# A Mamba layer's side work in single steps: tanh for sigmoid, packed norm factors, gates on GpSimd

## The chip, the cores and the metric

One Trainium2 chip, one of its cores. A core has five engines that run side by side, each with an instruction queue of its own that is worked off in order: PE (matmuls), DVE (vector work), ACT (table functions with a scale and a bias), POOL (GpSimd, general elementwise work) and SP (here for DMAs). They meet through semaphores: an instruction waits until a counter has reached a value. PSUM is the memory that PE writes, in eight banks of 128 rows by 512 fp32; SBUF is the working memory. The metric is the device time of one execution of the whole program, in microseconds (us); the median over several runs counts.

## The reference, cut to what matters

The model has five parts in a row over 2048 tokens of width 128: a gated feed-forward part, a Mamba layer, the feed-forward part again, a mixture of experts, attention, and the experts again. Only the Mamba layer is touched:

```python
hs = layernorm(x)                              # first norm, no weights; the residual too
proj = layernorm(hs) * ln_w + ln_b             # second norm
proj = proj @ in_proj_w + in_proj_b
x1, gate = split(proj, [E])                    # E = 256
x1 = silu(causal_conv(x1, conv_w) + conv_b)    # 4 taps
dt_r, B, C = split(x1 @ x_proj_w, [64, 80])    # rank 64, 16 states
dt = softplus(dt_r @ dt_proj_w + dt_proj_b)
h_t = exp(dt_t * A) * h_{t-1} + dt_t * B_t * x1_t      # for each of 16 states
y_t = sum_n h_t[n] * C_t[n] + x1_t * D
out = (sigmoid(gate) * y) @ out_proj_w + out_proj_b + hs
x = x + out
```

## The kernel before

**Layout.** Channels lie on the 128 partitions and time on the free axis. There are 2 batches of 1024 tokens (SEQ), so 2048 columns, cut into NCH = 4 chunks of 512 (COLS, and HALF within a batch). E = 256 is EB = 2 blocks of 128. The stage is `mamba`, which hands each engine its own list: `mamba_pe`, `mamba_act`, `mamba_dve`, `mamba_pool`. Their order is written out by hand; an engine waits for the others by `wait_ge` on the events named at the top of the file.

**Prelude.** PE forms each chunk's mean (with `mean_mat`, a matrix of 1/128) and DVE subtracts it (`m.hs`). ACT squares, PE forms the variance, the same in all 128 rows. Both norms come from that one variance. For each chunk and each norm ACT takes Ln, Exp (scale -0.5) and Square, and DVE runs a correction step: `second_norm` gives `m.xn`, the input of the projection, and `first_norm` adds the normed residual and the output bias into `c.x`. Batch 0 is then brought through projection, convolution (block 0 as four diagonal matmuls on PE, block 1 as multiply-adds on DVE), SiLU, the rank product (dt's rank, B and C), dt, gate, and the softplus of its block 0. MB_PREP lists these 512-wide products, 16 for batch 0. `first_norm` of chunks 2 and 3 runs on DVE after the first scan.

**Loop.** MB_ITEMS = 64 items: 2 batches x 2 blocks x 16 states. For item i:

```python
# PE:   B of the state spread to 128 rows (b_ps), C likewise in two halves (c_ps, one bank)
# DVE:  u_ps = dtx * b_ps                    (mb_input, L878)
# ACT:  d_a = exp(dt * neg_a)                (mb_decay, L696), two items ahead; copies C (L686)
# DVE:  state = scan(d_a, u_ps)              (mb_scan, L894)
# POOL: state = state * C                    (mb_hc, L920)
# PE:   y_ps += identity @ state             (mb_y, L557), two items later
```

b_ps is single, so PE may spread B of item i+1 only when DVE has multiplied item i; c_ps is one bank, so each half of C waits until ACT has copied the half before. Four decays and four states are held. Between these MB_TICKS places batch 1's products, all in bank 3; a convolution's four taps are spread over three items. Side work of ACT: x, conv, rank, dt and gate outputs (`x_out`, `conv_out`, `rank_out`, `z_out`, `gate_out`), SiLU of batch 1 at item 17, softplus at items 1, 25 and 31 (Abs and Exp, then Ln an item later), the sigmoid of a batch's gate at items 8 and 32. Silu and Sigmoid are in other tables than Exp and Ln, so a table load stands before and after them. POOL forms e - ((1 + e) - 1) and adds it to the logarithm; DVE then adds max(z, 0) (L885) and POOL multiplies dt by x (L916). After 16 items y of a block is complete: DVE's `drain` adds x * D into y_ps (L809) and multiplies by the gate (L813), after which PE may start the next y. `project_out` and `add_out` bring batch 0 out at items 35 to 38.

**Tail.** The last drain, two projections with two matmuls each, and two additions.

## Time and profile before

| | |
|---|---|
| median of 3 runs | 2078.65 us (2077.84 to 2080.35) |
| the profiled execution | 2083.6 us, its span 2082.3 us |
| busy in the span | PE 1859.7, DVE 1396.5, ACT 1128.0, POOL 1168.7 us |
| mean granted TensorE clock | 0.96 of full speed |
| Mamba stage | 161.05 to 505.83 us of the span |

The profile is of one execution. Times of its rows are us from the start of the span; a group gives the mean of one instruction in ns. An engine that is 89% busy over the program may still wait in one stage, so the stage is read by itself. Matmul durations are modelled and overlap: the distance of two starts is the better measure. `x2` at a matmul of fp32 is one product in two passes.

### The profile page before, as it was taken

Reading aid. Unit: us, or ns where it says so; the run is one execution under the profiler, and the core shown is the slowest. Engines: PE = TensorE matmul, PEld = TensorE weight load, DVE = VectorE, ACT = ScalarE, POOL = GpSimd, SP = SyncE. Lnnn points to the kernel's source line nnn. Section 1 sums busy time; section 2 is a strip of 40 time slices with the busy share of each in tenths; the row PEclk is TensorE's granted clock in tenths of the full one; section 3 lists DMA queues with packets and bytes.
Section 4 is the critical chain, followed back from the end, with each engine's and each line's share of the span. In section 5 each row is a group of like instructions: output and inputs, shape, how many; then the busy total and the mean of one; then the engine's idle time right before and its main releaser. Section 6 shows DMA issues by size and latency. Waiting matters only on the chain. (4 is left out here: it accounts for less than half of the span.)

```text
span 2082.3 us, 21845 instructions
## 1 busy us (share of the span) xinstructions
PE 1859.7 (89%) x7336; PEld 1308.0 (63%) x7336; DVE 1396.5 (67%) x2215; ACT 1128.0 (54%) x1586; POOL 1168.7 (56%) x645
## 2 busy tenths in 40 slices
PE   6996788776997994899999999999999999998588
PEld 3773343332775663677777777777777777775366
DVE  5426878896535763567777777777777777774376
ACT  4327667653434444565666566666665666653344
POOL 2450647763543553266666666666666666668354
...
GB/s 91 0 1 0 0 0 1 0 1 0 0 1 45 1 23 82 78 38 75 38 75 42 70 47 66 54 59 54 59 70 43 70 43 68 42 11 11 50 6 16
DMA packets 46048, 74.51 MB, mean 36 GB/s; under 512 B 26864, under 2 KB 28528, under 8 KB 45680
## 3 DMA queue, kind: packets, MB, share of 16 engines
...
q0 software_dynamic: 32, 0.00, 0.0%
...
## 5 line engine op out<-in xcount | busy, mean ns | idle before, releaser
L1994 POOL TENSOR_TENSOR at_e_lo<-at_e,at_e_hi 128x1024 fp32r<-128x1024 f32 x256 | 613.6, 2397 | 381.6 <-DVE at_e_hi L1961 378.8
L1819 ACT ACTIVATE at_e<-at_ps 128x1024 f32<-128x1024 f32 x256 | 263.1, 1028 | 284.3 <-PE at_ps L1726 284.3
L1811 ACT ACTIVATE at_ps<-at_ps,at_neg_diag 128x1024 f32<-128x1024 f32 x256 | 278.6, 1088 | 89.4 <-DVE at_neg_diag L1879 89.4
L1886 DVE TENSOR_REDUCE at_row_max<-at_ps 128x1 f32<-128x1024 f32 x256 | 311.2, 1216 | 5.7 <-PE at_ps L1707 5.7
L1961 DVE CAST at_e_hi<-at_e 128x1024 fp32r<-128x1024 f32 x256 | 257.5, 1006 | 36.9 <-ACT at_e L1819 36.7
L1879 DVE CUSTOM_DVE_ANT_0 at_junk_diag<-at_ps,ident 128x128 bf16<-128x128 f32 x256 | 74.1, 290 | 261.5 <-PE at_ps L1680 261.5
L920 POOL TENSOR_TENSOR mb_work<-mb_work,mb_c 128x1024 f32<-128x1024 f32 x64 | 152.0, 2375 | 147.9 <-DVE mb_work L894 147.1
L386 POOL TENSOR_TENSOR ffn_lo<-ffn_hid,ffn_hi 128x512 fp32r<-128x512 f32 x96 | 124.5, 1298 | 181.7 <-DVE ffn_hi L313 181.7
L1678 PE MATMUL at_ps<-at_k,at_q 128*128 128x512 f32 x512 | 162.9, 400 | 18.8 <-DMA at_k<-at_qk_lo 12.9
L1739 PE MATMUL at_pv_ps<-at_e_hi,at_v_hi 128*128 128x512 f32 x512 | 176.1, 425 | 0.3 <-ACT at_pv_sb L1835 0.3
L1707 PE MATMUL at_ps<-at_k,at_q 128*128 128x512 f32 x512 | 163.5, 401 | 11.5 <-DVE at_row_max L1886 8.1
L1745 PE MATMUL at_pv_ps<-at_e_lo,at_v_hi 128*128 128x512 f32 x512 | 161.8, 397 | 10.1 <-POOL at_e_lo L1994 9.9
L1723 PE MATMUL at_ps<-at_q,at_k 128*128 128x512 f32 x512 | 160.2, 394 | 0.0
L1680 PE MATMUL at_ps<-at_k,at_q 128*128 128x512 f32 x512 | 160.2, 394 | 0.0
L1726 PE MATMUL at_ps<-at_q,at_k 128*128 128x512 f32 x512 | 159.7, 393 | 0.0
L1741 PE MATMUL at_pv_ps<-at_e_hi,at_v_lo 128*64 128x512 f32 x512 | 159.5, 392 | 0.0
L557 PE MATMUL mb_y_ps<-mb_work,ident 128*128 128x512 f32 x256 | 137.9, 624 | 14.1 <-DVE mb_dtx L813 10.5
L894 DVE TENSOR_TENSOR_SCAN mb_work<-mb_work,mb_u_ps 128x1024 f32<-128x1024 f32 x64 | 146.3, 2286 | 5.1
L313 DVE CAST ffn_hi<-ffn_hid 128x512 fp32r<-128x512 f32 x96 | 56.5, 590 | 137.4 <-ACT ffn_hid L287 136.0
L1332 POOL TENSOR_TENSOR moe_hid_lo<-moe_prod,moe_hid_hi 128x512 fp32r<-128x512 f32 (+1 forms) x72 | 92.8, 1290 | 96.2 <-ACT moe_hid_hi L1164 96.2
L686 ACT ACTIVATE mb_c<-mb_c_ps 128x512 f32<-128x512 f32 x128 | 76.3, 596 | 94.1 <-PE mb_c_ps L546 93.3
L1745 PEld LDWEIGHTS at_pv_ps<-at_e_lo,at_v_hi 128*128 128x128 f32 x512 | 94.8, 188 | 51.2 <-POOL at_e_lo L1994 18.4
...
## 6 DMA issues: line engine op xcount, KB each, us to landing
...
```

The costliest lines, as they stand in the source:

```text
L1678: pe.eng.matmul(ps[:, HALF[hf]], q[:, CROSS, rows], k[:, CROSS, HALF[hf]], start=True, stop=False)
L1680: mm = pe.eng.matmul(ps[:, HALF[hf]], q[:, MAIN, rows], k[:, MAIN, HALF[hf]], start=False, stop=True)
L1707: mm = pe.eng.matmul(ps[:, HALF[hf]], q[:, MAIN, blk * P:(blk + 1) * P], k[:, MAIN, HALF[hf]], start=True, stop=True)
L1723: pe.eng.matmul(ps[:, HALF[hf]], k[:, CROSS, keys], q[:, CROSS, HALF[hf]], start=True, stop=False)
L1726: mm = pe.eng.matmul(ps[:, HALF[hf]], k[:, MAIN, keys], q[:, MAIN, HALF[hf]], start=False, stop=True)
L1739: pe.eng.matmul(m.pv_ps[:, HALF[hf]], with_ones, m.e_hi[e % 3][:, HALF[hf]], start=(blk == 0), stop=False)
L1745: mm = pe.eng.matmul(m.pv_ps[:, HALF[hf]], with_ones, m.e_lo[e % 3][:, HALF[hf]], start=False, stop=(blk == BLK - 1))
L1811: act.eng.activation(ps[:], ps[:], ACT.Exp, scale=SCALE, bias=m.small["neg_diag"][s][:, blk:blk + 1], accum_out=m.small["sums"][s][:, blk: ...
L1819: act.eng.activation(m.e[e % 2][:], slot("turned_scores", h, blk)[:], ACT.Exp, scale=SCALE).then_inc(sem["at_exp"])
L1886: dve.eng.tensor_reduce(m.small["row_max"][h % SLOTS][:, blk:blk + 1], slot("best", h, blk)[:], AX.X, ALU.max).then_inc(sem["at_best_out"])
L1961: dve.eng.tensor_copy(m.e_hi[e % 3][:], m.e[e % 2][:]).then_inc(sem["at_hi"])
L1994: pool.eng.tensor_tensor(m.e_lo[e % 3][:], m.e[e % 2][:], m.e_hi[e % 3][:].bitcast(F32), ALU.subtract).then_inc(sem["at_lo"])
```

## The change

- **Norms.** The variance matrix becomes two (`m.pack`), each with 1/128 in 32 columns for the first norm's rows and 32 for the second's; a pair of chunks so lands in one bank, 32 rows each for two chunks and two norms, with an epsilon a row (`m.norm_eps`). ACT takes Ln, Exp and Square once a pair, DVE corrects twice a pair, and PE spreads a row of the result to 128 rows with a selection matrix (`m.sel`, `spread_factor`, event mb_factor). POOL sets these matrices. One DVE step a chunk then gives xn, one the normed residual, kept in `m.hs`. ln_w is multiplied into in_w, and ln_b goes through in_w by four one-column matmuls into in_b. All first norms are in the prelude.
- **Residual.** `project_out` adds `m.hs` by an identity matmul, waited for less than the gated product; `add_out` adds the bias.
- **Batch 0.** Half 1 of block 0's convolution moves from PE to DVE, which works in halves; the logs and the softplus are in halves too. Its four gate products move to items 25 to 28 (MB_TICKS entries now carry the batch).
- **SiLU of batch 1.** Each conv output is Identity, Tanh of half, and a scaling by 0.5 plus 0.5, on ACT, and the product on POOL (MB_SILU).
- **Gate.** Tanh (items 41 to 44) and scaling (45 to 48) by block on ACT; POOL multiplies in halves (`gate_block`, MB_GATE). `drain` is one DVE operation, and y waits for it alone (mb_skip).
- **Tables.** The set that holds Exp and Tanh is loaded at items 5 and 40, the one with Exp and Ln at 17.
- **Softplus.** z_out writes |z| and max(z, 0); 1 + e and 1 - (1 + e) are ACT steps in items of their own, the three sums are POOL's.
- **y** is added three items behind the scan instead of two (MB_Y_LAG); the rest of B and C is formed behind the scan.

```diff
+MB_Y_LAG = 3
...
+    0: (1, 0, None), 1: (1, 1, None), 2: (1, 2, None), 3: (1, 3, None),
...
+    17: (1, 8, None), 19: (1, 9, None), 21: (1, 10, None), 22: (1, 11, None),
+    25: (0, 11, None), 26: (0, 12, None), 27: (0, 13, None), 28: (0, 14, None),
+    29: (1, 12, None), 30: (1, 13, None), 31: (1, 14, None), 32: (1, 15, None), 33: (1, 16, None), 34: (1, 17, None),
 }
-MB_SILU_TICK = 17
-MB_SOFTPLUS_TICK = {1: (0, 1), 25: (1, 0), 31: (1, 1)}
-MB_SIGMOID_TICK = {8: 0, 32: 1}
...
+MB_EXP = {3: (0, 1), 23: (1, 0), 36: (1, 1)}
+MB_ONE_PLUS = {5: (0, 1), 24: (1, 0), 37: (1, 1)}
+MB_ROUNDING = {6: (0, 1), 24: (1, 0), 38: (1, 1)}
+MB_LN = {4: (0, 1), 25: (1, 0), 39: (1, 1)}
+MB_SUMS = ({6: (0, 1), 24: (1, 0), 39: (1, 1)}, {8: (0, 1), 26: (1, 0), 41: (1, 1)}, {10: (0, 1), 28: (1, 0), 43: (1, 1)})
+MB_DTX = {13: (0, 1), 29: (1, 0), 45: (1, 1)}
+MB_SILU = {11: (0, 0), 12: (0, 1), 14: (1, 0), 16: (1, 1)}
+MB_TANH_TABLE, MB_LOG_TABLE = (5, 40), (17,)
+MB_TANH = {41: (0, 0), 42: (0, 1), 43: (1, 0), 44: (1, 1)}
+MB_SIGMOID = {45: (0, 0), 46: (0, 1), 47: (1, 0), 48: (1, 1)}
+MB_GATE = {48: (0, 0), 50: (0, 1), 54: (1, 0)}
+MB_PROJECT = {52: 0, 54: 1}
...
+        pe.eng.matmul(m.var_ps[ch // 2], m.pack[:, ch % 2, :], m.squares[ch],
+                      start=(ch % 2 == 0), stop=(ch % 2 == 1)).then_inc(sem["mb_var"])
...
+        pe.eng.matmul(m.factor_ps[n], m.sel[:, 2 * second + ch % 2, :], m.factor[ch // 2],
...
-            pe.wait_ge(sem["mb_gated"], EB * b + eb)
+            pe.wait_ge(sem["mb_skip"], EB * b + eb)
...
-        pe.wait_ge(sem["mb_gated"], EB * (b + 1))
...
+        pe.eng.matmul(ps, c.ident[:], m.hs[:, COLS[2 * b + h]], start=True, stop=False)
+        pe.wait_ge(sem["mb_gated"], 2 * EB * b + 3 + h)
         for eb in range(EB):
...
+            mm = pe.eng.matmul(ps, c.out_w[:, eb, :], m.dtx[b][:, eb, HALF[h]], start=False, stop=(eb == EB - 1))
...
+    for k in range(2 * EB):
+        mm = pe.eng.matmul(m.banks[7][:, k:k + 1], c.in_w[:, k * P:(k + 1) * P], c.ln_b[:, 0:1], start=True, stop=True)
+    mm.then_inc(sem["mb_mean"])
+    for ch in range(3):
...
+    for ch in range(2):
+        variance(ch)
+    pe.eng.matmul(m.banks[3], c.mean_mat[:], c.x[:, COLS[3]], start=True, stop=True).then_inc(sem["mb_mean"])
+    for ch in range(2, NCH):
+        variance(ch)
+    pe.wait_ge(sem["mb_start"], 2)
+    for n in range(2):
+        spread_factor(n)
...
+        act.eng.activation(m.inverse[pair], m.var_ps[pair], ACT.Ln, bias=m.norm_eps[:, 0:1]).then_inc(logs)
...
+        act.eng.activation(m.inverse[pair], m.inverse[pair], ACT.Exp, scale=-0.5).then_inc(logs)
...
+        act.eng.activation(m.factor[pair], m.inverse[pair], ACT.Square).then_inc(logs)
...
+        act.eng.activation(m.xs[1][:, eb, HALF[h]], mb_bank(m, 1, p), ACT.Identity, bias=c.conv_b[:, eb:eb + 1]).then_inc(out)
+        act.eng.activation(sigmoid, mb_bank(m, 1, p), ACT.Tanh, scale=0.5, bias=m.half_conv_b[:, eb:eb + 1]).then_inc(out)
+        act.wait_ge(out, at + 2)
+        act.eng.activation(sigmoid, sigmoid, ACT.Identity, scale=0.5, bias=0.5).then_inc(out)
...
+        act.eng.activation(m.e_of[g][:, HALF[h]], ps, ACT.Abs, bias=c.dt_b[:, eb:eb + 1]).then_inc(sem["mb_abs"])
+        act.eng.activation(m.dt[b][:, eb, HALF[h]], ps, ACT.Relu, bias=c.dt_b[:, eb:eb + 1]).then_inc(sem["mb_z_out"])
...
+        act.eng.activation(m.dtx[b][:, eb, :], m.e_of[g], ACT.Identity, bias=1.0).then_inc(sem["mb_logs"])
...
+        act.eng.activation(m.dtx[b][:, eb, :], m.dtx[b][:, eb, :], ACT.Identity, scale=-1.0, bias=1.0).then_inc(sem["mb_logs"])
...
+        if i in MB_TANH:
...
-            act.eng.activation(m.gate[b][:], m.gate[b][:], ACT.Sigmoid).then_inc(sem["mb_sigmoid"])
-            load_logs(act)
+            act.eng.activation(m.gate[b][eb], m.gate[b][eb], ACT.Tanh, scale=0.5).then_inc(sem["mb_sigmoid"])
...
+            act.eng.activation(m.gate[b][eb], m.gate[b][eb], ACT.Identity, scale=0.5, bias=0.5).then_inc(sem["mb_sigmoid"])
...
+        dve.eng.scalar_tensor_tensor(m.factor[pair], m.var_ps[pair], m.norm_eps[:, 0:1], m.factor[pair],
+                                     ALU.add, ALU.mult).then_inc(done)
...
+        dve.eng.scalar_tensor_tensor(m.factor[pair], m.factor[pair], 3.0, m.inverse[pair],
+                                     ALU.subtract, ALU.mult).then_inc(done)
...
-        dve.eng.scalar_tensor_tensor(m.xn[:, COLS[ch]], m.hs[:, COLS[ch]], -0.5, m.sq2[ch], ALU.mult, ALU.mult).then_inc(done)
...
-        dve.eng.tensor_scalar(m.xn[:, COLS[ch]], m.xn[:, COLS[ch]], c.ln_w[:, 0:1], c.ln_b[:, 0:1],
...
+        dve.eng.scalar_tensor_tensor(m.xn[:, COLS[ch]], m.hs[:, COLS[ch]], -0.5 * (1.0 + EPS) ** -0.5,
+                                     m.factor_ps[ch], ALU.mult, ALU.mult).then_inc(sem["mb_xn"])
...
+        dve.eng.scalar_tensor_tensor(m.hs[:, COLS[ch]], m.hs[:, COLS[ch]], -0.5, m.factor_ps[NCH + ch],
+                                     ALU.mult, ALU.mult).then_inc(sem["mb_first_norm"])
...
-        dve.eng.scalar_tensor_tensor(m.y_ps[:], m.xs[b][:, eb, :], c.d_skip[:, eb:eb + 1], m.y_ps[:],
+        dve.eng.scalar_tensor_tensor(m.dtx[b][:, eb, :], m.xs[b][:, eb, :], c.d_skip[:, eb:eb + 1], m.y_ps[:],
...
-        dve.eng.tensor_tensor(m.dtx[b][:, eb, :], m.y_ps[:], m.gate[b][:, eb, :], ALU.mult).then_inc(sem["mb_gated"])
...
-        dve.eng.tensor_tensor(c.x[:, COLS[ch]], c.x[:, COLS[ch]], m.c_ps if b and h else m.banks[3],
...
+        dve.eng.scalar_tensor_tensor(c.x[:, COLS[ch]], m.c_ps if b and h else m.banks[3], c.out_b[:, 0:1],
+                                     c.x[:, COLS[ch]], ALU.add, ALU.add).then_inc(sem["x_mamba"])
...
+    for n, (eb, h) in enumerate(((1, 0), (1, 1), (0, 1))):
+        convolve(n, eb, h)
...
+        part = HALF[h]
...
+        dve.eng.tensor_scalar(soft[:, part], m.e_neg[:, part], 1.0, -1.0, ALU.add, ALU.add).then_inc(log1p)
...
+        dve.eng.tensor_tensor(soft[:, part], m.e_neg[:, part], soft[:, part], ALU.subtract).then_inc(log1p)
...
+        dve.eng.tensor_tensor(dt[:, part], dt[:, part], soft[:, part], ALU.add).then_inc(log1p)
+        first_norm(2 + h)
...
-            dve.eng.scalar_tensor_tensor(dt, dt, 0.0, m.log1p, ALU.max, ALU.add).then_inc(sem["mb_dt"])
-        if n == 2 and i > STATES:
-            drain(*mb_part(i - 3)[0:2])
...
+        if n == 3 and i > STATES:
+            drain(*mb_part(i - 4)[0:2])
...
-        if i == 0:
-            for ch in range(2, NCH):
-                first_norm(ch)
+        if (at := mb_product_due(i, 1)) and MB_PREP[at[0]][at[1]][0] == "rank":
+            rest_of_bc(*at)
...
+        for h in range(2):
+            pool.eng.tensor_tensor(m.dtx[b][:, eb, HALF[h]], m.dtx[b][:, eb, HALF[h]], m.gate[b][eb][:, HALF[h]],
+                                   ALU.mult).then_inc(sem["mb_gated"])
...
-            pool.eng.tensor_scalar(m.dtx[b][:, eb, :], m.e_neg, 1.0, -1.0, ALU.add, ALU.add).then_inc(soft)
...
+            pool.eng.tensor_tensor(m.dtx[b][:, eb, :], m.e_of[g], m.dtx[b][:, eb, :], ALU.add).then_inc(soft)
...
+            pool.eng.tensor_tensor(m.dt[b][:, eb, :], m.dt[b][:, eb, :], m.dtx[b][:, eb, :], ALU.add).then_inc(soft)
...
-            pool.eng.tensor_tensor(m.log1p, m.log1p, m.dtx[b][:, eb, :], ALU.add).then_inc(soft)
+            pool.eng.tensor_tensor(m.dt[b][:, eb, :], m.dt[b][:, eb, :], m.log_of[g], ALU.add).then_inc(soft)
...
+            pool.eng.tensor_tensor(m.xs[1][:, eb, HALF[h]], m.xs[1][:, eb, HALF[h]], sigmoid,
+                                   ALU.mult).then_inc(sem["mb_silu"])
...
+    gate_block(BATCH - 1, EB - 1)
```

## Rows read from the trace of the kernel before

**Rows 1.** Table of stretches, whole kernel: start:end, length, then each engine's busy time.

```profile
161.05:209.63 48.58, 33.45 (x67) 13.64 (x67) 33.28 (x53) 38.05 (x57) 2.76 (x3) 0.87 0.00 1
209.63:492.60 282.97, 230.93 (x577) 107.09 (x577) 248.60 (x147) 173.30 (x231) 180.88 (x75) 0.92 0.00 0
492.60:505.83 13.23, 8.13 (x14) 2.69 (x12) 3.89 (x4) 0.00 (x0) 2.34 (x1) 0.87 0.00 0
```

**Rows 2.** DVE's timeline, the loop: start, duration, instruction, idle before it and its releaser.

```profile
209.63 1.23 DVE L878 TENSOR_TENSOR mb_u_ps<-mb_dtx,mb_b_ps 128x1024 f32<-128x1024 f32 x1 [4.89 <-PE mb_b_ps L534]
...
219.42 1.22 DVE L878 TENSOR_TENSOR mb_u_ps<-mb_dtx,mb_b_ps 128x1024 f32<-128x1024 f32 x1
...
242.09 1.23 DVE L878 TENSOR_TENSOR mb_u_ps<-mb_dtx,mb_b_ps 128x1024 f32<-128x1024 f32 x1
...
249.47 1.23 DVE L878 TENSOR_TENSOR mb_u_ps<-mb_dtx,mb_b_ps 128x1024 f32<-128x1024 f32 x1
...
267.71 1.23 DVE L878 TENSOR_TENSOR mb_u_ps<-mb_dtx,mb_b_ps 128x1024 f32<-128x1024 f32 x1 [3.51 <-PE mb_b_ps L534]
...
294.21 1.23 DVE L878 TENSOR_TENSOR mb_u_ps<-mb_dtx,mb_b_ps 128x1024 f32<-128x1024 f32 x1
...
303.88 1.23 DVE L878 TENSOR_TENSOR mb_u_ps<-mb_dtx,mb_b_ps 128x1024 f32<-128x1024 f32 x1 [3.80 <-PE mb_b_ps L534]
...
346.94 1.23 DVE L878 TENSOR_TENSOR mb_u_ps<-mb_dtx,mb_b_ps 128x1024 f32<-128x1024 f32 x1
...
356.64 1.23 DVE L878 TENSOR_TENSOR mb_u_ps<-mb_dtx,mb_b_ps 128x1024 f32<-128x1024 f32 x1
...
368.75 1.23 DVE L878 TENSOR_TENSOR mb_u_ps<-mb_dtx,mb_b_ps 128x1024 f32<-128x1024 f32 x1
...
378.16 1.23 DVE L878 TENSOR_TENSOR mb_u_ps<-mb_dtx,mb_b_ps 128x1024 f32<-128x1024 f32 x1 [0.89 <-PE mb_b_ps L534]
...
399.91 1.23 DVE L878 TENSOR_TENSOR mb_u_ps<-mb_dtx,mb_b_ps 128x1024 f32<-128x1024 f32 x1
...
403.62 1.23 DVE L878 TENSOR_TENSOR mb_u_ps<-mb_dtx,mb_b_ps 128x1024 f32<-128x1024 f32 x1
...
437.04 1.23 DVE L878 TENSOR_TENSOR mb_u_ps<-mb_dtx,mb_b_ps 128x1024 f32<-128x1024 f32 x1
...
443.80 1.23 DVE L878 TENSOR_TENSOR mb_u_ps<-mb_dtx,mb_b_ps 128x1024 f32<-128x1024 f32 x1 [0.89 <-PE mb_b_ps L534]
```

**Rows 3.** Waits of DVE in the loop: us in total, times, longest.

```profile
DVE mb_u_ps L878 <- PE mb_b_ps L534: 20.6, 13, 4.9
```

**Rows 4.** PE's timeline, the loop and the tail.

```profile
281.41 1.02 PE L509 MATMUL mb_c_ps<-mb_conv_in,mb_conv_diag 128*128 128x512 f32 x2
...
285.00 1.02 PE L509 MATMUL mb_c_ps<-mb_conv_in,mb_conv_diag 128*128 128x512 f32 x2
...
423.46 0.73 PE L534 MATMUL mb_b_ps<-mb_bc,pick_r 128*128 128x512 f32 x2 [0.71 <-DVE mb_u_ps L878]
...
440.87 2.04 PE L557 MATMUL mb_y_ps<-mb_work,ident 128*128 128x512 f32 x2 [4.10 <-DVE mb_dtx L813]
...
499.69 5.40 PE L573 MATMUL mb_c_ps<-mb_dtx,out_w 128*128 128x512 f32 x8 [2.64 <-DVE mb_dtx L813]
```

**Rows 5.** Groups of instructions in the loop: busy us, mean ns, idle before.

```profile
L920 POOL TENSOR_TENSOR mb_work<-mb_work,mb_c 128x1024 f32<-128x1024 f32 x63 | 149.6, 2375 | 146.6 <-DVE mb_work L894 145.8 <-ACT mb_c L686 0.8
...
L673 ACT ACTIVATE mb_e_neg<-mb_dt 128x1024 f32<-128x1024 f32 x3 | 3.1, 1049 | 0.0
...
L651 ACT ACTIVATE mb_xs<-mb_c_ps,conv_b 128x512 f32<-128x512 f32 x4 | 2.7, 683 | 0.0
```

**Rows 6.** Groups of instructions in the prelude.

```profile
L781 DVE SCALAR_TENSOR_TENSOR mb_xn<-mb_gate,mb_work 128x512 f32<-128x512 f32 x4 | 2.8, 691 | 0.1
```

**Rows 7.** ACT's timeline, the prelude.

```profile
181.28 1.28 ACT L713 ACT_TABLE_LOAD   x1
182.58 0.69 ACT L713 ACTIVATE mb_xs<-mb_y_ps,conv_b 128x512 f32<-128x512 f32 x1
```

More of the change, by code:

```diff
@@ L464, in mb_part, with mb_log_at @@
+MB_GATE = {48: (0, 0), 50: (0, 1), 54: (1, 0)}
+MB_PROJECT = {52: 0, 54: 1}
+def mb_product_due(i, lag=0):
+    b, p, taps = MB_TICKS.get(i - lag, (None, None, ()))
+    return (b, p) if taps is None or TAPS - 1 in taps else None
+def mb_log_at(b, eb, step):
+    order = sorted((i, n) for n, ticks in enumerate((MB_EXP, MB_ONE_PLUS, MB_ROUNDING, MB_LN))
+                   for i, part in ticks.items() if part == (b, eb))
+    return 4 * (b * EB + eb) + 1 + [n for _, n in order].index(step)
 def mb_part(i):
@@ L467, in mb_part, with mb_last_of_bank @@
     return (*divmod(be, EB), n)
+def mb_last_of_bank(bank, p):
+    return max((k for k in range(p) if MB_BANKS0[k] == bank), default=None)
 def mb_emptied(b, p):
@@ L493, in product @@
         ps = mb_bank(m, b, p)
-        before = (b, p - (1 if b else 4))
-        if b and p == 0:
-            before = 0, max(k for k in range(len(MB_PREP[0])) if k % 4 == 3)
-        if before[1] >= 0:
-            event, count = mb_emptied(*before)
-            pe.wait_ge(sem[event], count)
+        if (b, p) in MB_IN_BANK3[1:]:
+            emptied(*MB_IN_BANK3[MB_IN_BANK3.index((b, p)) - 1])
+        elif (before := mb_last_of_bank(MB_BANKS0[p], p)) is not None:
+            emptied(0, before)
         if kind in ("x", "gate"):
@@ new lines, in mamba_act @@
+    for n, (eb, h) in enumerate(((1, 0), (1, 1), (0, 1))):
+        act.wait_ge(sem["mb_conv_dve"], (n + 1) * TAPS)
+        act.eng.activation(xs[:, eb, HALF[h]], xs[:, eb, HALF[h]], ACT.Silu).then_inc(sem["mb_xs"])
+    load_logs(act)
+    for p in range(5, 7):
+        rank_out(0, p)
+    for h in range(2):
+        z_out(0, 7 + h)
+        act.wait_ge(sem["mb_abs"], h + 1)
+        act.eng.activation(m.e_neg[:, HALF[h]], m.e_neg[:, HALF[h]], ACT.Exp, scale=-1.0).then_inc(sem["mb_logs"])
+    for h in range(2):
+        act.wait_ge(sem["mb_logs"], h + 1)
+        act.eng.activation(m.log1p[:, HALF[h]], m.e_neg[:, HALF[h]], ACT.Ln, bias=1.0).then_inc(sem["mb_logs"])
@@ new lines, in convolve @@
+    def convolve(n, eb, h):
+        conv, out = sem["mb_conv_dve"], m.xs[0][:, eb, HALF[h]]
+        dve.wait_ge(sem["mb_x_out"], 2 * h + 2 - eb)
+        dve.wait_ge(sem["mb_pick"], 2)
+        taps = [m.conv_in[:, eb, k + h * CH:k + (h + 1) * CH] for k in range(TAPS)]
+        dve.eng.tensor_scalar(out, taps[0], c.conv_w[:, eb, 0:1], c.conv_b[:, eb:eb + 1], ALU.mult, ALU.add).then_inc(conv)
+        for k in range(1, TAPS):
+            dve.wait_ge(conv, n * TAPS + k)
+            dve.eng.scalar_tensor_tensor(out, taps[k], c.conv_w[:, eb, k:k + 1], out, ALU.mult, ALU.add).then_inc(conv)
@@ L871, in mamba_dve @@
+    for h in range(2):
+        dve.wait_ge(log1p, 3 * h + 3)
+        dve.wait_ge(sem["mb_logs"], 2 + h + 1)
+        dve.eng.tensor_tensor(dt[:, HALF[h]], dt[:, HALF[h]], m.log1p[:, HALF[h]], ALU.add).then_inc(log1p)
+    dve.wait_ge(log1p, 8)
+    dve.eng.tensor_tensor(soft, dt, m.xs[0][:, 0, :], ALU.mult).then_inc(log1p)
+    dve.wait_ge(log1p, 9)
+    dve.wait_ge(sem["mb_norm"], 4)
+    dve.wait_ge(sem["mb_first_norm"], NCH)
+    dve.wait_ge(sem["mb_factor"], 2 * NCH)
     for i in range(MB_ITEMS):
```

455 lines of the change are left out of this document (231 added, 224 removed), and 6 rows, old and new, of the table MB_TICKS.

## Prediction

> **What bounds it now.** First the table of stretches [rows 1]: the Mamba stage is 344.8 us of the 2082.3 (prelude 48.6, loop over 64 items 283.0, tail 13.2); the diff touches nothing else and no DMA. In the loop DVE is busy 248.6, PE 230.9, ACT 173.3, POOL 180.9. Next, DVE's timeline [rows 2]: an undisturbed item starts 3.71 after the one before (399.91 to 403.62), and 64 of them are 237.4. The loop takes 282.97, 45.6 more. Taking 3.71 an item from the differences of those starts shows where: item 0 6.1, items 1 to 5 4.1, item 6 3.7, items 7 to 10 3.4, 11 to 17 0.5, 18 6.0, 19 to 29 2.2, 30 6.0, 31 to 33 1.0, 34 5.7, 35 to 39 3.2, 40 to 49 nothing, 50 3.0, 51 to 63 0.6. Then DVE's waits [rows 3]: 20.6 of it is B's broadcast from PE; most of the rest is DVE's own extra work. Last, PE's timeline [rows 4]: in a plain item PE idles 0.71 before it may overwrite B, and with one extra fp32 matmul its round is 3.59 (281.41 to 285.00). So DVE bounds the loop, PE is second with little room, POOL and ACT matter where they hold one of these up. The prelude is a chain through all four engines.
>
> **The loop, part by part** (excesses from the timeline [rows 2]).
> Removed: (a) item 0's 6.1: two first norms behind the first scan, now in the prelude. (b) At items 6, 30 and 36 DVE adds the softplus parts; with late decays and POOL's dtx behind the second these are 3.7, 7.0 and, of the 3.2 at 35 to 39, 1.5. POOL takes them: -12.2. (c) At item 10 DVE waits 3.51 for B: PE stood behind ACT's copies of C, those behind the sigmoid and its two table loads, 4.5 on ACT. Tanh needs none between decays: -3.4. (d) A drain is two DVE operations of some 1.25, and PE's next y waits for both. The three cost 6.0 (with SiLU's two loads and a rank product), 6.5 (with a late y) and 3.4. DVE keeps one operation, 1.2 over the floor.
> Left of the drains: before the third, PE idled 4.10 and then ran a matmul pair in 2.04, where 285.00 shows 1.02 [rows 4]; B came 0.89 late. The idle becomes 2.9. If the clock holds, a drain costs 1.2, and 2.1 at item 19, where a rank product of two matmuls stands before B; if it drops as now, 1.1 more, and at item 19 another 2.3. I take the drop, the nearest shown case: 4.4, 2.3, 2.3 = 9.0, bounds 4.5 and 9.0.
> Start-up: items 1 to 5 cost 4.1; ACT will again copy x, and exp, ln, 1+e and the tanh load come at items 3 to 5: 3, bounds 1 and 6.
> Convolution: 16 diagonal matmuls of 0.85 in items 4 to 15. PE's round with two is 4.45, with one 3.59, so twelve items need 1.7 more than DVE, which PE's lead takes, as now (0.5 at items 11 to 17). New on ACT: each of the four outputs is three operations of 0.6 to 0.69 where one was 0.68 [rows 5], ahead of a copy of C that PE needs only after the next product and B. Within the 3.
> The rest of B and C (0.72 twice, 2.2 now with its waits) moves behind the scan: 1.4. project_out gets the residual as a third matmul, so PE's rounds 52 and 54 are 2.74 + 2.55 = 5.3; three rounds need 13.3 where DVE gives 11.1: 2.2, DVE's two additions inside, bounds 1.3 and 4.
> Batch 0's four gate products now lie in items 25 to 28, rounds of 3.59 under DVE's 3.71; without that cover 3.4.
> Softplus on ACT: 1+e and its rounding are two more steps of 1.05 [rows 5] a block; tanh and its scaling are four each. ACT's plain item takes 2.3 of 3.71, a copy of C may come some 2 late. Only items 5 and 24 get more than that: 1.0, bounds 0 and 5.
> POOL: sums of 2.36, as before but for one of 3.6; new are four SiLU halves (1.3) and the gates (2.6 a block). It has 3.71 - 2.38 = 1.33 free an item [rows 5]; the worst pile (items 11 to 14) makes it 1.7 late, and with MB_Y_LAG 3 y asks for its product one item later. Nothing.
> Left over the floor: 9.0 + 3 + 1.4 + 2.2 + 1.0 = 16.6 instead of 45.6. **Loop -29.0.**
>
> **The prelude.** Counted from 161.05 with 0.72 a DVE half step [rows 6], 0.66 an ACT half step and 1.28 a table load [rows 7], 0.9 an fp32 matmul. The four bias products are eight weight loads, some 1.6; one-column matmuls are not in the trace, so the bounds are nothing and 3.6 (four full ones). Means and centres then come 0.8 later; the fourth mean stands behind two variances, its centre ends at 168.7, the eight diagonals at 170.6. Ln, Exp, Square of the first pair are done at 169.1, under them. POOL's twelve memsets ahead of the spreading, at 0.92 each (2.76 for three [rows 1]), end by 172.1. Two factor steps end 172.0, spreading 172.95, xn of chunks 0 and 1 173.7 and 174.6, the second factor 176.0, three half convolutions of 2.7 (0.5 and three of 0.73) 184.1. SiLU of the last half 184.8, table 186.1, two rank outputs 188.5, Abs, Relu and Exp of both halves 192.0. DVE has first norms 0 and 1 done at 191.55, behind PE's spreads and dt products. Two halves of softplus with a first norm each, 2.56 a half, end 196.7, two log additions 198.1, dt times x 199.4. B is there by 193.5. PE stands idle several times before that, and after such a stretch a pair takes twice as long [rows 4]: I add 0.9. Item 0 starts at 200.3 against 209.63: **prelude -9.3**, bounds -13 (ACT's and DVE's halves overlap fully) and -4 (half clock in every spread and rank product, bias products at 3.6). What goes is four gate products ahead of B (4.89 of waiting before the first multiply [rows 2]), a convolution on PE, and 24 ACT half steps of the norms, now six.
>
> **The tail.** Drain 1.28, then POOL's first gate half 1.3 instead of DVE's 1.22. The residual matmul of half 0 is hidden by them, that of half 1 is not: +0.9. But the idle before the projections shrinks from 2.64 to 1.9, and their eight passes, 5.40 now [rows 4], are 3.5 at full clock. Bounds -1.0 and +1.9, I take +0.5.
>
> **Table loads against the notes.** A load of 1.28 is followed by its ACTIVATE 1.30 after its own start [rows 7]. The Trainium skill, "ScalarE: Activation LUTs", section "What ACT_TABLE_LOAD costs", adds a drain of 1380 ns to each switch, 2.66 us in all. The trace disagrees: nothing lies between. By the page the loop's loads, six now and three after, would be worth another 4.1 us of ACT.
>
> **Sum.** -29.0 - 9.3 + 0.5 = -37.8. The profiled execution took 2083.6 (span 2082.3) and would take 2045.8. It lies 4.95 above the median of 2078.65, so the median becomes 2040.9, rounded to 2041.
>
> **Rivals.**
> *ACT in part exposed.* The 4.5 block of item 10 was exposed by 3.4, so 1.1 fits unnoticed. The four conv outputs (1.9), items 5 (2.3) and 24 (2.1), and pairs with x, dt or gate outputs (1.6) exceed that. Where PE has no lead each loses up to 1.2, eight of them 10: 2051. For: PE's round of 3.59. Against: items 19 to 29 hold single steps of 1.05 now and are 2.2 over, 2.1 of it the rank items.
> *The prelude does not shorten* by more than 1: it gets three more PE round trips (variance pair, factor, spread). 2049.
> *ACT fully exposed, slower.* Between the copies of C stand 20 wide steps of 1.06 (21.2), the conv outputs (7.4), and x, dt, gate, rank outputs and loads (17.7): 46.3. If each delays C, so B, so DVE by its whole length, less the 4 counted above, it is 2041 + 42 = 2083. It decides when 38 of the 46 are exposed, so only if PE never regains a lead; plain items give 0.71 each.
> *Loads come back.* If each tanh draws its own load and each decay the other, as silu and sigmoid do now, 8 groups x 2 x 1.28 = 20.5 on ACT, some 12 exposed: 2053. Against: Silu's four in a row draw one.
> *Less left over.* The clock holds at the drains and ACT hides: 4.5 + 1 + 1.4 + 1.3 = 8.2 over the floor (loop -37.4), prelude -11, tail +0.5: 2031.
>
> **How the numbers follow.** Forecast 0.70 (its own range 2034 to 2048), ACT in part 0.10, prelude 0.05, loads 0.03, less left over 0.06, ACT fully exposed 0.04, and 0.02 for a sum of these that comes out level. A measurement here tells 0.2%, 4 us, from no change. Faster 0.94, same 0.02, slower 0.04. The range takes in the less-left-over and the partly exposed cases: 2030 to 2054.
>
> **What would show it.** Right: the first multiply some 39 after the stage's start; a loop near 254; plain items at 3.71; no log1p addition on DVE in the loop; lone table loads at items 5, 17 and 40; waits for B below 10. Wrong: DVE waiting for B in most items of 4 to 16 and 23 to 48 with ACT the releaser of C; scans waiting for y (lag 3, four states held); the half clock for longer than now.

## The result, and the profile after

The new kernel takes 2041.18 us, median of 4 runs (2039.14 to 2043.06), the old one 2079.5 beside it: a ratio of 0.9816, 95% interval 0.98 to 0.9831. Forecast were 2041 and 2030 to 2054. The table of stretches of the new kernel (columns as in [rows 1]), prelude, loop and tail:

```profile
159.10:198.46 39.36, 32.44 (x76) 13.82 (x76) 28.26 (x53) 25.50 (x39) 5.38 (x15) 0.94 0.00 1
198.46:452.54 254.08, 225.76 (x587) 105.83 (x588) 230.90 (x135) 182.19 (x251) 188.96 (x85) 0.97 0.00 0
452.54:465.06 12.52, 8.34 (x19) 2.98 (x17) 2.78 (x4) 0.00 (x0) 4.82 (x3) 1.00 0.00 0
```

Against [rows 1] the prelude is 9.2 shorter (forecast 9.3), the loop 28.9 (29.0), the tail 0.7 (0.5 longer). Together the stage is 38.8 shorter in the two profiled executions; the medians lie 38.3 apart. DVE's work in the loop fell by 17.7 and its waits for B from 20.6 [rows 3] to 11.4 ("below 10" was one of the signs named for being right: that one missed); ACT's and POOL's work grew by 9 and 8, and both are still less busy than DVE. DVE's waits in the loop:

```profile
DVE mb_u_ps L980 <- PE mb_b_ps L595: 11.4, 12, 2.3
DVE mb_u_ps L980 <- DVE mb_work L989: 0.9, 2, 0.5
DVE mb_work L989 <- PE mb_y_ps L616: 0.6, 3, 0.3
```

Take 3.71 an item from the differences of the multiplies' starts, as before. The excess is 16.6, as forecast, but otherwise divided:

| items | forecast | measured |
|---|---|---|
| 0 to 17 (start-up, convolution) | 3 | 5.8 |
| 19, 35, 51 (drains) | 9.0 | 2.3 + 1.8 + 1.8 = 5.9 |
| 18, 20 (rest of B and C) | 1.4 | 1.3 |
| 52 to 55 (output) | 2.2 | 2.9 |
| others | 1.0 | 0.7 |

An item is counted from its own multiply to the next one. 2.3 of the first line is one item, 7. DVE's timeline there, then PE's and ACT's of the same time:

```profile
226.09 1.23 DVE L980 TENSOR_TENSOR mb_u_ps<-mb_dtx,mb_b_ps 128x1024 f32<-128x1024 f32 x1
...
232.12 1.23 DVE L980 TENSOR_TENSOR mb_u_ps<-mb_dtx,mb_b_ps 128x1024 f32<-128x1024 f32 x1 [2.33 <-PE mb_b_ps L595]
```

```profile
224.81 1.03 PE L595 MATMUL mb_b_ps<-mb_bc,pick_r 128*128 128x512 f32 x2
226.01 0.50 PE L606 MATMUL mb_c_ps<-mb_bc,pick_r 128*128 128x512 f32 x1 [0.17 <-ACT mb_c L784]
...
227.53 0.50 PE L606 MATMUL mb_c_ps<-mb_bc,pick_r 128*128 128x512 f32 x1 [0.17 <-ACT mb_c L784]
...
229.64 1.98 PE L548 MATMUL mb_c_ps<-mb_conv_in,mb_conv_diag 128*128 128x512 f32 x4 [0.75 <-ACT mb_e_neg L736]
231.06 1.03 PE L595 MATMUL mb_b_ps<-mb_bc,pick_r 128*128 128x512 f32 x2
```

```profile
223.00 1.05 ACT L766 ACTIVATE mb_dtx<-mb_dt 128x1024 f32<-128x1024 f32 x1
224.07 1.28 ACT L112 ACT_TABLE_LOAD   x1
225.36 0.60 ACT L784 ACTIVATE mb_c<-mb_c_ps 128x512 f32<-128x512 f32 x1
...
226.89 0.59 ACT L784 ACTIVATE mb_c<-mb_c_ps 128x512 f32<-128x512 f32 x1
227.37 1.06 ACT L770 ACTIVATE mb_dtx<-mb_dtx 128x1024 f32<-128x1024 f32 x1
228.32 0.69 ACT L735 ACTIVATE mb_xs<-mb_c_ps,conv_b 128x512 f32<-128x512 f32 x1
228.89 0.70 ACT L736 ACTIVATE mb_e_neg<-mb_c_ps,mb_half_conv_b 128x512 f32<-128x512 f32 x1
```

Read backwards: the multiply waits for B (L595); B stands on PE behind the second convolution's first matmuls (L548); these wait for bank 3, which ACT empties with the second step of the first output (L736); and that step comes late behind the rounding (L770). Before that, PE had stood twice in front of a half of C (L606), because ACT copies the half before (L784) late behind 1+e (L766) and the table load.

How much is whose follows from the distance of two B's. At item 10, where PE waits for nobody, it is 4.53 with a product of two matmuls:

```profile
238.26 1.03 PE L595 MATMUL mb_b_ps<-mb_bc,pick_r 128*128 128x512 f32 x2
...
241.41 1.95 PE L548 MATMUL mb_c_ps<-mb_conv_in,mb_conv_diag 128*128 128x512 f32 x4
242.79 1.02 PE L595 MATMUL mb_b_ps<-mb_bc,pick_r 128*128 128x512 f32 x2
```

At item 7 it is 6.25, so 1.7 more: by the starts between, some 0.8 at the two halves of C and 0.9 at the bank. The other 0.6 of item 7, and the 0.6 of items 10 and 13, are PE's own round of 4.53 against DVE's 3.71; rounds with one matmul, 3.60, give PE only 0.1 of lead each. Item 4's 0.6 is such a round with a wait of 0.17 for ACT; item 17's comes with the rank product's two matmuls, PE waiting 0.5 and 0.2 for copies of C before them; item 1's 0.9 falls where PE, after an idle of 4.1, runs at a granted clock of 0.50 (199.0 to 206.5).

The drains: PE's timeline at items 19 and 35, the y pair behind the drain, what stands between, and B.

```profile
278.13 1.10 PE L616 MATMUL mb_y_ps<-mb_work,ident 128*128 128x512 f32 x2 [1.14 <-DVE mb_dtx L913]
279.06 1.88 PE L558 MATMUL mb_c_ps<-mb_xs,x_w 128*128 128x512 f32 x4
280.38 1.03 PE L595 MATMUL mb_b_ps<-mb_bc,pick_r 128*128 128x512 f32 x2
...
340.68 2.05 PE L616 MATMUL mb_y_ps<-mb_work,ident 128*128 128x512 f32 x2 [2.84 <-DVE mb_dtx L913]
341.74 1.84 PE L595 MATMUL mb_b_ps<-mb_bc,pick_r 128*128 128x512 f32 x2
```

At 35 (and 51) the idle is the 2.9 forecast and the pair takes 2.05: the granted clock from 340.5 to 343.5 is 0.50, the lower level, 1.2 GHz. At 19 PE came late itself, idled only 1.14, and the clock held: 1.00, 2.4 GHz, from 277.9 to 281.4. The four other profiles with 1.14 to 1.18 of idle before such a y (softplus earlier, PE kept busy, lag 2, gates ahead of B) had the pair at full speed too.

### The profile page after: what moved, and what is told of

It reads as the page before. It is cut to its first block and busy times, and to the rows that moved or that the text cites. A ratio compares the mean times of both kernels' runs of the same rounds, so it can differ in the third digit from the quotient of the medians.

```text
span 2037.7 us, 21921 instructions
## 1 busy us (share of the span) xinstructions
PE 1844.3 (91%) x7360; PEld 1301.5 (64%) x7360; DVE 1374.8 (67%) x2202; ACT 1124.5 (55%) x1587; POOL 1183.9 (58%) x669
## 3 DMA queue, kind: packets, MB, share of 16 engines
HBM read 20.93 MB, written 1.18 MB: 11 GB/s over the span
## 5 line engine op out<-in xcount | busy, mean ns | idle before, releaser
L1944 ACT ACTIVATE at_e<-at_ps 128x1024 f32<-128x1024 f32 x256 | 263.0, 1028 | 281.4 <-PE at_ps L1851 281.4
L390 POOL TENSOR_TENSOR ffn_lo<-ffn_hid,ffn_hi 128x512 fp32r<-128x512 f32 x96 | 124.6, 1300 | 173.0 <-DVE ffn_hi L317 173.0
L616 PE MATMUL mb_y_ps<-mb_work,ident 128*128 128x512 f32 x256 | 131.9, 602 | 8.3 <-DVE mb_dtx L913 6.8
L1803 PEld LDWEIGHTS at_ps<-at_k,at_q 128*128 128x128 f32 x512 | 95.2, 189 | 47.2 <-DMA at_k<-at_qk_lo 14.9
```

Source lines behind the costliest of these rows:

```text
L1803: pe.eng.matmul(ps[:, HALF[hf]], q[:, CROSS, rows], k[:, CROSS, HALF[hf]], start=True, stop=False)
L1944: act.eng.activation(m.e[e % 2][:], slot("turned_scores", h, blk)[:], ACT.Exp, scale=SCALE).then_inc(sem["at_exp"])
```

## The experiments

Each changes the new kernel only as its diff says. The loop's length, from each trace, is the finest measure, but not a perfect one. Of items that no edit reaches most repeat within 0.1 from kernel to kernel; items 1 to 4 together (1.5 in the new kernel, 1.2 in most, 0.05 in "drain twice") and items 35, 36, 51 and 52 (by up to 0.9 each) move with PE's clock (last section). The new kernel's loop is 254.1, and that of "PE kept busy", whose edit does not reach the loop, 253.6: a difference of 0.5 says nothing.

**Loads back** (the rival "Loads come back").

```diff
+        load_tanh(act)
         act.eng.activation(sigmoid, mb_bank(m, 1, p), ACT.Tanh, ...)
+        load_logs(act)
...
```

The same stands around the gates' tanh; the loads at items 5, 17 and 40 are gone.

> The new kernel, with each of the eight tanh steps (four in the convolution's outputs, four on the gates) preceded by a load of tanh's table set and followed by a load of the decays' set: 16 loads of 1.28 us and none of the three at items 5, 17, 40, so 13 more, 16.6 us of ScalarE. Theory A (ScalarE's long work in the batch-1 convolution is exposed, as item 7's 2.33 us of waiting for B shows; from item 41 on ScalarE has 1.4 us free in each item and a gate tanh alone takes 1.05): the four convolution groups become 1.9 + 2.56 = 4.5 us long, and each costs about 2 more, the gates' groups 3.6 us long in consecutive items and some 4 in all: the loop 254.1 becomes 266, the run about 2053, as the rival in the prediction has it. Theory B (PE's lead hides it, only blocks above 4.5 us show): the loop grows by under 4, the run is 2041 to 2045.

Measured: 2058.38 us, ratio 0.9897 (0.9881 to 0.9914), loop 272.8: 18.7 longer, more than the 16.6 of ACT added. Items 7, 10, 13, 17 cost 4.5, 2.1, 2.1, 4.7, item 19 4.0, items 43 to 46 7.4. ACT's time is exposed almost one for one wherever its item is full. Item 17 adds to it: PE waits 3.18 there for a copy of C behind the last conv output, and its matmuls behind that idle, and again behind the one of 2.43 at item 19, run partly at the lower clock (granted 0.59 and 0.66). PE never waits for POOL in this loop. The rival's price, 12, was too low.

**Softplus earlier**, to thin out the pile before item 7.

```diff
-MB_EXP = {3: (0, 1), ...};  MB_ONE_PLUS = {5: (0, 1), ...}
+MB_EXP = {2: (0, 1), ...};  MB_ONE_PLUS = {3: (0, 1), ...}
```

> The new kernel with ScalarE's softplus exp of the first block at item 2 instead of 3 and its 1+e at item 3 instead of 5; the tanh table load stays at item 5. Theory A (item 7's excess of 2.32 us is ScalarE's pile of 1.05 + 1.28 + 1.06 + 1.9 us in items 5 to 7, which holds up the copies of C, so B): item 7's excess falls to 1.0 or less, items 1 to 4 may gain up to 0.6, items 0 to 17 together cost 4.3 over the floor instead of 5.84, the run is 1.5 us shorter. Theory B (it is PE's own work in items 4 to 7, convolution matmuls ahead of B, or the four convolution operations): item 7 stays at 2.2 or more and the run at 2041.

Measured: 2039.8, ratio 0.9809 (0.9792 to 0.9825), loop 253.5, which is no shorter than with no edit in it (253.6). Item 7 fell from 2.3 to 1.5, item 4 rose by 0.4. Between the two: at item 7 PE no longer waits for a copy of C, but still 0.74 for the bank, because the rounding still stands before the output. So 1+e had cost 0.8 by way of C; the rest is the bank and PE's own round.

**B before y** at the drains.

```diff
+        late = i >= STATES and n == 3
-        if i >= MB_Y_LAG:
+        if i >= MB_Y_LAG and not late:
             add_to_y(i - MB_Y_LAG, 0)
...
             spread_b(i + 1)
             spread_c(i + 1, 1)
+        if late:
+            add_to_y(i - MB_Y_LAG, 0)
```

> The new kernel with PE's order changed at items 19, 35 and 51 alone: the next item's B and C go ahead of the first half of y, which has to wait for DVE's drain there. Theory A (DVE waits 1.26, 0.89 and 0.89 us for B behind y at the three drains, and PE's half clock matters only for what DVE waits for): these waits go, each drain costs 1.2 to 1.3 (its own DVE operation and start), the loop is 2.5 to 3.0 shorter, 251.3. Theory B (PE's two halves of y then collide with the next round and the wait moves to the next item's B or to the scan's wait for y): the three drains together stay at 5 or more of 6.0 and the run at 2041.

Measured: 2036.2, ratio 0.9792 (0.9776 to 0.9808), loop 249.3, 4.8 shorter. Items 19, 35, 51 cost 1.1, 1.0, 1.0, so 2.7 less, as Theory A says, and item 52 fell from 1.8 to 0.3, which it had not seen. That is 4.3 for the edit; the other 0.5 lies in items 1 and 4, which it doesn't reach. PE's timeline at item 35 of this kernel:

```profile
337.62 0.73 PE L595 MATMUL mb_b_ps<-mb_bc,pick_r 128*128 128x512 f32 x2 [1.56 <-DVE mb_u_ps L983]
...
338.89 3.17 PE L616 MATMUL mb_y_ps<-mb_work,ident 128*128 128x512 f32 x4 [0.31 <-DVE mb_dtx L916]
```

The y's at 35 still run slow (3.17 for four records, 1.88 at item 19), but the B that DVE needs next is no longer behind them.

**PE kept busy** in the prelude.

```diff
     for ch in range(2, NCH):
         variance(ch)
+        pe.wait_ge(sem["mb_centred"], 2)
+        pe.eng.matmul(m.banks[1], c.mean_mat[:], c.x[:, COLS[1]], start=True, stop=True)
```

> The new kernel with two extra matmuls in the prelude, one behind each of the last two variances, into a bank that nobody needs then: they fill PE's idle stretches of 0.90 and 0.99 us ahead of the first spreading matmuls, which in the new kernel took 3.44 us for a pair and at other places 1.88. Theory A (the pair is slow because the clock had fallen to its lower level after PE's idle stretches, which the extra work prevents): the pair takes about 1.9, the first normed chunk is ready 0.6 to 0.9 earlier and the loop's first multiply comes about 1 us earlier. Theory B (the clock is low there whatever PE does, or something else holds it): the pair stays at 3.4, the extra work adds up to 0.4, the first multiply is at the same place or later.

Measured: 2041.08, ratio 0.9813 (0.9797 to 0.983); first multiply 37.88 after the stage's start, 39.36 in the new kernel. But two of the three kernels above, which don't have the edit, showed 37.9 too, and the median is that of the new kernel, so this run alone decides nothing (last section).

**Product behind B**, and then **outputs behind C** on top of it.

```diff
-        if i in MB_TICKS:
-            product(*MB_TICKS[i])
...
             spread_b(i + 1)
             spread_c(i + 1, 1)
+        if i in MB_TICKS:
+            product(*MB_TICKS[i])
```

> The new kernel with PE's order changed in every item that has a batch-1 product: the product (x, convolution, rank, dt, gate) is issued behind B and the second half of C for the next item, where it stood ahead of them. Theory A (what is left of items 7, 10, 13 and 17, 1.54 + 0.6 + 0.6 + 0.6 with softplus moved and 2.32 + 0.6 + 0.6 + 0.6 without, is B standing behind a product that waits for bank 3 until ScalarE has read the last convolution): these four items cost 0.3 or less each, the rank items 0.65 as now (DVE's own operation), item 19's drain loses the 0.85 of the rank product, the loop is 4 to 5 shorter, 249.5. Theory B (PE's round has no room: B now comes as before but the product pushes the second y and the next round by the same time): the excess moves one item on, the loop stays within 1 of 254.1.

> As the kernel before in this group (PE's product behind B), and ScalarE's output steps of those products (x, three convolution steps, rank, dt, gate) moved from ahead of the item's two copies of C to behind them. Theory A (C's copies late behind ScalarE's output steps still hold PE up, by 0.3 to 0.6 at items 1, 4 and 10): a further 1 to 1.5 us goes from items 0 to 17 and the loop is 248. Theory B (the copies were in time once the product no longer stood ahead of B; the outputs come later instead, and rank's and dt's chains with them): same or up to 1 longer, the rank items 18 and 20 above all, where DVE waits for the rank output behind its scan.

Measured: the first 2039.57, ratio 0.9809 (0.9792 to 0.9825), loop 253.3; the second 2067.62, ratio 0.9947 (0.9931 to 0.9964), loop 284.3. The first turned waits for B into waits for y. DVE's waits in it:

```profile
DVE mb_work L989 <- PE mb_y_ps L616: 7.6, 8, 2.0
...
DVE mb_u_ps L980 <- PE mb_b_ps L595: 3.4, 5, 1.7
```

Item 7's 2.3 became 1.9 at item 8, items 10 and 13 moved to 11 and 14, and item 20 went from 0.65 to 2.4: Theory B. PE never waits for bank 3 in this kernel; what is left is its round, and at item 8 a wait of 1.0 for a copy of C behind ACT's output. In the second neither theory's number holds, the loop is 31.0 longer than in the first: ACT's output now waits behind C, the next product behind the output (PE waits 24.9 for bank 3, in 17 places), y behind the product, and DVE waits 29.8 for y in 18 items. Bank 3 is one buffer for all these products; here its round trip is the limit, and the outputs' place first in ACT's item is what keeps it short.

**Sums on DVE**: the three softplus additions of each block taken from POOL to DVE, at the same items (6, 8, 10; 24, 26, 28; 39, 41, 43), between multiply and scan; the second and third likewise.

```diff
+        if i in MB_SUMS[0]:
+            b1, eb1 = MB_SUMS[0][i]
+            dve.wait_ge(sem["mb_logs"], mb_log_at(b1, eb1, 2))
+            dve.eng.tensor_tensor(m.dtx[b1][:, eb1, :], m.e_of[b1 * EB + eb1], m.dtx[b1][:, eb1, :], ALU.add)...
```

> The new kernel with the three sums of softplus of the three blocks in the loop back on DVE, nine operations of 128x1024 between multiply and scan at the items where GpSimd did them (6, 8, 10; 24, 26, 28; 39, 41, 43). Theory A (the prediction's: a DVE operation costs its own 1.22 plus 0.05 of issue, PE and ScalarE catch up meanwhile): 9 x 1.27 = 11.4 longer at most, less what hides in item 10's excess of 0.6, the loop 264 to 265.5, the run 2052. Theory B (a DVE operation from SBUF alone runs slower while GpSimd works, as the 2.79 us of one such operation in the kernel before): 20 or more, the loop 274, the run 2061. Theory C (the sums were not what cost time, the waits beside them were): under 6.

Measured: 2060.77, ratio 0.9911 (0.9894 to 0.9927), loop 276.2, 22.1 longer. That is Theory B's size, but only in part by its mechanism. 8.6 is waiting for ACT's rounding before two of the nine operations, which no theory named and which POOL has time for; those two took 1.22 each. The other seven took 2.28 to 2.30 and made their items 2.0 longer than the floor. That is 24.8 in nine items; 4.5 goes off because PE catches up at items 7, 10, 13, 17 and 29, 2.2 comes on at 36 and 52, and 0.3 goes off in items 0 to 4. DVE's timeline at items 6 and 8, then POOL's:

```profile
228.90 1.22 DVE L984 TENSOR_TENSOR mb_dtx<-mb_dt,mb_dtx 128x1024 f32<-128x1024 f32 x1 [4.85 <-ACT mb_dtx L770]
...
237.28 2.30 DVE L989 TENSOR_TENSOR mb_dt<-mb_dt,mb_dtx 128x1024 f32<-128x1024 f32 x1
```

```profile
236.11 2.38 POOL L1034 TENSOR_TENSOR mb_work<-mb_work,mb_c 128x1024 f32<-128x1024 f32 x1 [1.35 <-DVE mb_work L1003]
```

With POOL idle (from 225.15 to 232.40) the addition takes 1.22; issued in the middle of a POOL operation it takes 2.30 and ends at 239.58, 1.09 behind POOL's end at 238.49.

**Lag 2**: `MB_Y_LAG = 2`, and the drains at `n == 2`.

> The new kernel with MB_Y_LAG 2, as the old one had it, and the drains on DVE at the third item of a block instead of the fourth (items 18, 34, 50). Theory A (the prediction counts GpSimd's late products at nothing because y asks for them one item later; with lag 2 PE would wait for GpSimd behind every sum of 2.36 us, 12 times some 1.0, and behind SiLU, dtx and gate steps): the loop is 6 to 15 longer. Theory B (GpSimd's spare 1.33 us an item covers it, lag 2 would do): within 1.5 of 254.1.

Measured: 2040.02, ratio 0.9814 (0.9797 to 0.983), loop 253.2, Theory B: PE waited for POOL twice, 1.8 together. POOL's pile was rightly counted at nothing, but POOL's spare time covers nearly all of it without the longer lag.

**B first, softplus spread**: the edits of "B before y" and "PE kept busy", with

```diff
-MB_ONE_PLUS = {5: (0, 1), ...};  MB_ROUNDING = {6: (0, 1), ...};  MB_DTX = {13: (0, 1), ...}
+MB_ONE_PLUS = {8: (0, 1), ...};  MB_ROUNDING = {9: (0, 1), ...};  MB_DTX = {14: (0, 1), ...}
...
```

and exp at item 2, POOL's sums at 9, 10, 12, its SiLU halves at 11, 13, 15, 16.

> The new kernel with three edits together: B and C ahead of y at items 19, 35, 51 (which alone took 4.8 us off the loop); the first block's softplus spread apart (exp at item 2, ln 4, the tanh load 5, nothing at 6, 1+e at 8, rounding at 9, GpSimd's sums at 9, 10, 12, its dtx at 14, its SiLU halves at 11, 13, 15, 16); and the two extra matmuls in the prelude. Theory A (item 7's 2.32 us is the first convolution output standing behind ScalarE's pile, PE's next convolution waiting for its bank with B behind it; GpSimd has room, as the kernel with lag 2 showed): item 7 costs at most 0.6, like items 10 and 13, items 0 to 17 together 3.6 to 4.0, the loop is 247.0 to 247.8, the run 2034.5. Theory B (PE waits for the bank there whatever ScalarE did before, since three operations of 1.9 us are longer than the item's room): item 7 keeps 1.5 and the loop 249. Theory C (GpSimd's sums now crowd): waits for y or copies of C behind GpSimd appear at items 12 to 17. For the prelude: if the extra matmuls keep PE's clock, the first multiply comes 37.9 after the stage's start; of the eight kernels profiled so far without them four showed 37.9 and four 39.4 to 39.6, with the same idle stretches, so one more 37.9 says little and a 39.5 says that they don't.

Measured: 2035.18, ratio 0.9792 (0.9779 to 0.9805), loop 249.3, no shorter than with B before y alone. Item 7 fell to 0.6, PE's own round, as Theory A says. But item 10, now behind 1+e and the rounding, rose to 1.5 (PE waits 0.74 for the bank, as it did at 7), and DVE waited for POOL's late dtx, as Theory C says, in its own timeline:

```profile
263.06 1.23 DVE L985 TENSOR_TENSOR mb_u_ps<-mb_dtx,mb_b_ps 128x1024 f32<-128x1024 f32 x1 [1.48 <-POOL mb_dtx L1048]
```

**Softplus spread again**: the same with exp at 1, 1+e at 2, rounding at 8, sums at 8, 9, 11, dtx at 13.

> The new kernel with B and C ahead of y at items 19, 35, 51, the two extra matmuls in the prelude, and the first block's softplus in another order than in the kernel that had 1+e at item 8 and rounding at 9: exp at item 1, 1+e at 2, ln 4, the tanh load 5, nothing at 6, rounding at 8, GpSimd's sums at 8, 9, 11, its dtx at 13 as in the new kernel, its SiLU halves at 12, 14, 15, 16. Theory A (item 7's excess is decided by what ScalarE does in items 5 and 6, item 10's by items 8 and 9, so item 7 stays at 0.6 as there and item 10, where 1.54 had come in, goes back to 0.6; with dtx one item earlier the wait of 1.5 us for it at item 16 goes): items 0 to 17 cost 3.8 to 4.4, the loop is 247.8 to 248.4, the run 2034. Theory B (a long step beside an x output in items 1, 2 and 4 is exposed like those of items 5 to 7): items 1 to 4 cost 1 or more in addition, and nothing is won over 249.3.

Measured: 2038.5, ratio 0.9804 (0.9787 to 0.982), loop 248.9. Items 7 and 10 cost 0.6 each and dtx is in time, but items 1 to 4 now cost 2.5 where they had cost 1.2: mostly Theory B. Items 0 to 17 cost 5.8, 5.2, 5.4 and 5.0 in the four placements of the softplus. In the first placement they cost 5.8, 5.4, 5.4 and 4.0 in four kernels whose edits don't reach them (the new one, B before y, PE kept busy, drain twice), so these sums don't rank the placements. What the single items show is that ACT's surplus goes where it is put.

**Drain twice**: DVE's drain operation done twice, y released by the second; with PE kept busy.

> The new kernel with DVE's drain operation done twice over (the same values), and y's release behind the second, so that each drain holds PE and DVE as long as the two operations of the old kernel did (and the two extra matmuls in the prelude). Theory A (the prediction's: with the longer idle PE's clock falls at every drain, 1.1 more at items 35 and 51 and 2.3 more at item 19 where a rank product stands before B): the three drains together go from 5.9 to 5.9 + 3.9 + 2 to 3 = 12 to 13; item 19 alone costs 5.5 to 6. Theory B (PE's idle only grows by the operation and the clock there is as it is): each costs 1.27 more on DVE and B comes that much later, so 5.9 + 3 x 1.27 = 9.7; item 19 costs 3.6.

Measured: 2050.42, ratio 0.9864 (0.9849 to 0.9879), loop 258.4. Items 19, 35, 51 cost 6.6, 2.3, 3.1, 12.0 together, and item 36 0.7: Theory A, with item 19 above its 5.5 to 6. The loop grew by less, because items 1 to 7 cost 1.4 less than in "PE kept busy": PE's clock rose earlier there, by 203 instead of some 207. PE's timeline at item 19:

```profile
278.11 2.04 PE L616 MATMUL mb_y_ps<-mb_work,ident 128*128 128x512 f32 x2 [2.46 <-DVE mb_dtx L918]
279.95 3.62 PE L558 MATMUL mb_c_ps<-mb_xs,x_w 128*128 128x512 f32 x4
282.58 1.79 PE L595 MATMUL mb_b_ps<-mb_bc,pick_r 128*128 128x512 f32 x2
```

The idle is 2.46 instead of 1.14, and all three behind it run at half speed (granted clock 0.50 from 278 to 284); DVE waited 4.25 for B, 1.26 in the new kernel. In the tail the idle before the projections was 3.17, they took 3.78 for the first half where the new kernel's took 1.98, and the tail was 16.9.

**Gates ahead of B**: batch 0's four gate products and outputs back in the prelude; with PE kept busy.

```diff
-    25: (0, 11, None), 26: (0, 12, None), 27: (0, 13, None), 28: (0, 14, None),
...
+    for p in range(11, 15):
+        product(0, p)
     spread_b(0)
```

> The new kernel with batch 0's four gate products back in the prelude, ahead of B's first broadcast on PE and ahead of the first copies of C on ScalarE, all four through one bank in turn; items 25 to 28 have no product any more (and the two extra matmuls in the prelude). Theory A (the prediction's: what stands ahead of B in the prelude is paid, what stands in items 25 to 28 is covered by DVE's 3.71): four products of 0.86 and three output steps of 0.68 between them, 5.5, less the 4 us that B had in hand before softplus ended, so the first multiply comes 2 to 5 later, and the loop stays at 254 or loses 0.2. Theory B (softplus on DVE hides them whole): under 1 later. Theory C (the loop pays for the gates today): the loop is more than 1 shorter.

Measured: 2044.54, ratio 0.9837 (0.9822 to 0.9852). The first multiply came at 38.8 instead of 37.9, 0.9 later and not 2 to 5, but its scan then waited 2.4 for its decay: 3.3 in all, which is Theory A's amount in another place (the medians differ by 3.5). Items 25 to 28 are 3.71 apart with the gates and without them, so the loop did hide them.

## Why the prediction was right

**The loop, -28.9 of -29.0 forecast**, is right as a sum and wrong in two terms that cancel.

*Start-up and convolution, 3 forecast, 5.8 measured.* Start-up took 1.0 (items 0 to 3), the convolution's items 4.1 and item 17 0.6. Two steps failed. The first is "which PE's lead takes, as now": PE has no lead to speak of, and a round with two matmuls costs 0.6 each of the four times, 2.4, without any help from ACT. In the old kernel these rounds showed as well, with 0.7 and 0.5 at items 4 and 13; item 6's 3.7 of DVE's own work let PE catch up for item 7, and item 10's round lay inside its 3.4. The second is "ahead of a copy of C that PE needs only after the next product and B. Within the 3": one half of C stands ahead of the product and B in PE's list, and the product itself waits for its bank behind ACT's output. At item 7 this cost 1.7, 0.8 by the copies and 0.9 by the bank. The rival "ACT in part exposed" expected eight places of up to 1.2; one came. Shown by the moved softplus: 1+e taken away from item 5 took the 0.8 away, the rounding taken away from item 6 the 0.9, and what stayed, 0.6, is what items 10 and 13 cost. That PE's round is the reason for these is read from the trace.

*Drains, 9.0 forecast, 5.9 measured.* The step that failed is "The idle becomes 2.9", taken for all three: at item 19 it is 1.14. There the clock held and 2.3 of the 4.4 came, near the 2.1 that the prediction gives for a held clock. At 35 and 51 each term was right but for 0.5: the drop cost 0.8, not 1.1, and the drain without it 1.0, not 1.2. Doubling the drain lengthened the idle and brought item 19's drop back at once, with 3.0 beyond the extra operation.

That these two cancel, 2.8 too little and 3.1 too much, is luck: nothing ties one to the other.

*Item 0's first norms and item 10's table loads, -6.1 and -3.4.* Item 0 now costs 0.1 and item 10 0.6. "Loads back" shows that loads among the decays do cost time; taking the norms out of the loop was not tested by itself.

*Moving the sums, -12.2.* Undone, it costs 22.1, of which 8.6 the old kernel would not have paid (it waited for no rounding on ACT). The 13.5 left is near the forecast, but the two are not the same sum: the 12.2 was read off the old items' excess, while the 13.5 is nine operations, seven of them stretched to twice their length beside POOL, less what PE catches up.

*Rest of B and C, output, gates under DVE's cover, POOL at nothing:* within 0.7 each; the gates and POOL are shown by experiment. Of the output's 2.9, item 52's 1.5 belonged to the y's of item 51, as "B before y" showed, which leaves 1.4 for the output itself, near its lower bound. Rest of B and C is only read from the trace.

**The prelude, -9.2 of -9.3.** The parts moved more than the sum: the eight bias matmuls took 1.05, not 1.6; POOL's memsets were done by 165.3; the two spreading matmuls ran at half speed, 3.44 for 1.96, so 1.5 where the prediction had 0.9. That 1.5 is not there in every execution (last section), and without it the prelude would be 10.7 shorter; so much of the nearness is chance. The gates' removal is worth 3.3 here, by experiment. The rest, the packed norms above all, is read from the trace, not tested.

**The tail, -0.7 where +0.5 was forecast**, but inside its bounds. PE idled 1.86 ahead of the first projections and they took 1.98 (granted clock 1.00 in the tail, 0.87 before), so the clock gave back all it could, where +0.5 had taken the middle of the bounds.

**Table loads.** Alone at items 5, 17, 40, as forecast. 13 more of them, 16.6 of ACT, cost 18.7, 1.4 each. The Trainium skill, "ScalarE: Activation LUTs", section "What ACT_TABLE_LOAD costs", adds a drain of 1.38 to each load. By that figure the 13 would have been some 35 of ACT (an estimate, 13 times 2.66). The trace disagrees: the load at 224.07 took 1.28, and the next ACTIVATE starts at 225.36.
